# Projection stage of a graph network: carried rows weighed in place, GpSimd without its wait for VectorE

## The reference

```
alpha = softmax over the edges of a node (per head, 8 heads of 32 features)
out   = segment_sum(xs[src] * alpha)            # [6250, 256]
out   = out @ Wo + bo + b
out   = layernorm(out) * lg + lb + x            # x: the layer's input
then  batch norm over the nodes: mean and variance of each column
```

## Time and profile before

| | us |
|---|---|
| median of 3 timed runs | 8060.63 (8050.53 to 8062.14) |
| span of the profiled execution (the page gives no time around it) | 8042.1 |
| busy: PE, DVE, POOL, ACT | 5804.3, 4583.5, 4597.4, 2363.1 |
| projection stage, layer 1, between 1566.5 and 1789.0 | 222.5 |
| projection stage, layer 2, between 3064.0 and 3276.5 | 212.5 |

### The profile page before, as it was taken

The page is one execution under the profiler, slowest core; times in us unless marked ns, Lnnn a source line. Parts: engine busy times, 40 slices in busy tenths (PEclk is TensorE's granted clock), DMA queues, the critical chain, the costliest instruction groups (busy, mean ns, idle before and its releaser), DMA issues. The chain is left out here.

```text
span 8042.1 us, 109715 instructions
## 1 busy us (share of the span) xinstructions
PE 5804.3 (72%) x22914; PEld 3937.3 (49%) x23071; DVE 4583.5 (57%) x9420; ACT 2363.1 (29%) x7394; POOL 4597.4 (57%) x4150
## 2 busy tenths in 40 slices
PE   3699989688999978577776998565565666666640
PEld 2365555356666655466666444444444433334320
DVE  4577777766777776734444222444457444444438
ACT  0366666245666642200000111000002222222212
POOL 0277777215777742077776000777761888888870
PEclk7799999788998877655555899777777888888875
DMA  1745455115454532311111333555542666666664
GB/s 49 173 133 136 134 137 135 54 57 168 134 135 135 135 88 60 91 31 31 31 31 28 105 121 118 134 131 131 131 112 77 68 69 69 68 69 68 68 95 159
DMA packets 537478, 783.86 MB, mean 97 GB/s; under 512 B 92084, under 2 KB 410117, under 8 KB 535966
## 3 DMA queue, kind: packets, MB, share of 16 engines
q0 software_dynamic: 269440, 489.53, 31.7%
q1 hardware_dynamic: 266542, 291.49, 11.9%
q10 hardware_dynamic: 1348, 1.21, 0.0%
HBM read 531.97 MB, written 249.93 MB: 97 GB/s over the span
## 5 line engine op out<-in xcount | busy, mean ns | idle before, releaser
L725 POOL DMA_INDIRECT at_x<-table,at_idx x1664 | 1590.7, 956 | 673.4 <-issue 516.5
L2545 POOL DMA_INDIRECT acc<-sc_rows,sc_idx x832 | 1355.6, 1629 | 298.1 <-DMA acc<-sc_rows,sc_idx 180.6
L1954 POOL DMA_INDIRECT rel_ring<-rel_table,rel_idx x784 | 741.0, 945 | 845.7 <-ACT rel_idx L2000 607.3
L800 PE MATMUL at_psO<-at_x,at_main 128*128 128x273 f32 x3328 | 1063.0, 445 | 125.6 <-DVE agg L990 123.4
L1797 POOL DMA_INDIRECT conv_x<-conv_table,conv_idx x784 | 755.5, 964 | 389.4 <-issue 238.6
L2585 PE MATMUL sc_psR<-gated,sc_pick 128*128 x1664 | 592.3, 452 | 459.9 <-ACTq L2623 457.0
L1982 PE MATMUL rel_psO<-rel_ring,rel_hot 128*128 x1664 | 606.3, 543 | 423.7 <-issue 217.0
L990 DVE TENSOR_TENSOR agg<-agg,at_psO 128x273 f32 x1664 | 726.8, 437 | 246.5 <-DVE agg L990 167.0
L800 PEld LDWEIGHTS at_psO<-at_x,at_main 128*128 128x128 f32 x3328 | 621.6, 205 | 496.4 <-issue 369.4
L1982 PEld LDWEIGHTS rel_psO<-rel_ring,rel_hot 128*128 128x128 f32 x1664 | 462.6, 285 | 567.8 <-issue 466.6
L2585 PEld LDWEIGHTS sc_psR<-gated,sc_pick 128*128 128x128 f32 x1664 | 296.1, 210 | 752.7 <-issue 743.9
(11 more groups left out here) (431 smaller groups left out, 9329.8 us busy)
## 6 DMA issues: line engine op xcount, KB each, us to landing
at_place<-places SPq DMA_DIRECT2D x208, 256.0 KB, 3.7
rel_table<-cr_rows SPq DMA_DIRECT2D x50, 1024.0 KB
at_x<-table,at_idx POOLq DMA_INDIRECT x1664
acc<-zeros SPq DMA_DIRECT2D x204, 128.5 KB
la_t<-acc SPq DMA_DIRECT2D x40, 642.5 KB
acc<-sc_rows,sc_idx POOLq DMA_INDIRECT x832, 3.9
pj_x<-table SPq DMA_DIRECT2D x20, 640.0 KB, 4.2
conv_x<-conv_table,conv_idx POOLq DMA_INDIRECT x784, 2.4
```

What stands on the lines that cost most here:

```text
L725: pool.indirect_dma_start(x[b][:, j, 0:TABW], None, d.table[0:NR, :], bass.IndirectOffsetOnAxis(ap=idx[b][:, j:j + 1], axis=0)).then_inc(x ...
L800: ins = nc.tensor.matmul(psO[j % BANKS][:, 0:AGG], main[b % 2][:, j, :], x[b][:, j, 0:AGG], start=True, stop=True)
L1954: pool.indirect_dma_start(x[:, at:at + D], None, d.rel_table[:, :], bass.IndirectOffsetOnAxis(ap=idx[r][:, j:j + 1], axis=0)).then_inc(x_r ...
L2545: pool.indirect_dma_start(d.acc[k][0:NR + P, :], bass.IndirectOffsetOnAxis(ap=idx[b][:, j:j + 1], axis=0), rows[b % 2][:, j, :], None, com ...
```

## The change

`s2` and `sq` are gone. The carried rows are multiplied in place, in the carried table, and POOL no longer waits for `sum_ready` ahead of them. L1371 adds the table's rows. The squares go into the table's first five rows and `mean` and `var` into two rows of its second chunk, which have been read by then. The waits ahead of the squares stay.

```
-        s2 = sb("s2", [P, CT, D])
-        sq = sb("sq", [P, CT, D])
...
-        mean, var = s2[:, 0, :], s2[:, 1, :]
         cg = cagg[:].rearrange("p (n k) -> p n k", k=AGG)
+
+        sq = cg[:, 0:CT, 0:D]
+        mean, var = cg[:, CT, 0:D], cg[:, CT + 1, 0:D]
...
                 def carried_rows(c):
-                    if c >= 1:
-                        pool.wait_ge(sum_ready, c)
-                    nc.gpsimd.tensor_tensor(heads(s2[:]), heads(cg[:, c * CT:(c + 1) * CT, 0:D]), f(c, 1), ALU.mult).then_inc(carried, 1)
+                    rows = heads(cg[:, c * CT:(c + 1) * CT, 0:D])
+                    nc.gpsimd.tensor_tensor(rows, rows, f(c, 1), ALU.mult).then_inc(carried, 1)
...
-                    v.tensor_tensor(s1[b][:], s1[b][:], s2[:], ALU.add).then_inc(sum_ready, 1)
+                    v.tensor_tensor(s1[b][:], s1[b][:], cg[:, cs, 0:D], ALU.add).then_inc(sum_ready, 1)
```

## The result

The changed kernel takes 8099.2 us (median of 4 runs, 8088.7 to 8100.4) where the kernel before takes 8061.0 (median of 4): **1.0046 of before, 95% interval 1.0031 to 1.0060**, slower by 38 us. In a second comparison it was 1.0052 (1.0038 to 1.0066), 41 us.

What follows compares the result with a forecast made beforehand. VectorE's sum was taken as the path, GpSimd's wait as slack. Meetings in weigh(4) to weigh(8) and long returns gave +25.1 a layer, +50.2 for two: span 8092.3, with 18.5 to the median 8111 us, range 8085 to 8140.

Steps and rivals of the forecast that it cites:

- The burst is hidden: Carried rows 2 to 5 run back to back from 1589.6 to about 1598.9; at most one VectorE operation loses 2.2, covered by 5 us.
- L1370 of before pays 2.57: In weigh(4) to weigh(8), a shift starting 4.46 after a finish makes this sum take 4.06, +2.57.
- The next sum pays 2.2: In weigh(4) to weigh(7), the carried row queued behind the shift goes ahead of L1371, which loses 2.2.
- rival A: In weigh, L1371 goes ahead of the waiting carried row, only the shift costs: +16.3 a layer, 8093; chance 0.14.
- D: Not slower: loads of h land 6.7 or more after a finish, shifts meet nothing, down to 8053; chance 0.08.
- Turn(20) at 1647.86: Layer 1: weigh(4) ends at 1647.86 instead of 1643.09, so this PE turn comes 3.26 late.
- Turn(25) at 1669.31: Layer 1: this PE turn follows the factors at 1652.99 by 11.55 + 4.77.
- Each return 6.19: From PE's turn over PE and ScalarE to VectorE's next factors: 6.19 every time, nearly all at 1.2 GHz.
- rival B: PE's clock stays at 2.4 GHz, each return but the last is 3.64: +14.9 a layer, 8090; chance 0.09.
- Turn(25): PE stands 4.1: Layer 1: PE would reach this turn at 1665.19 and stand 4.1, about the gap followed by half clock.
- Rival C: PE's clock doesn't come back, its tiles take 5.34 and set the pace: +46.3 a layer, 8153; chance 0.07.
- The 18.5 between the span and the median: The kernel before: timed median 8060.6 lies 18.5 above the profiled span; left as is and added to the forecast span.

## Why the prediction was right, and where it was off

The forecast was 8111, slower by 50; measured was slower by 38 and 41, and by 43.9 in the two stages of the profile. The mechanism came as forecast, and one term of the sum was too large. Of the 12 us between 8111 and 8099, 6.3 lie in the two stages; the rest is the distance between the stages of one execution and the medians, and isn't traced further. Step by step:

- *The wait is slack, the sum is the path*: held; with the wait in place the rest of the change makes no difference that shows.
- *The burst is hidden*: held. Its price fell on another operation than I thought: L1380, a small tensor_scalar, took 1.30 instead of 0.17 at 1600.67, and weigh(2) began 1.3 late. PE's turn(10) came without a wait.
- *L1370 of before pays 2.57*: held to 0.01 (4.06). *The next sum pays 2.2*: it pays 2.02 (3.51), and GpSimd goes first, as forecast; rival A falls. So does D, since the shifts of weigh(4) to weigh(8) start 4.27 to 5.14 after a finish, not 6.7.
- *Turn(20) at 1647.86*: it came at 1650.96 on this trace's clock, 3.11 late from the start, so 1647.85. *Turn(25) at 1669.31*: 1669.17.
- *Each return 6.19*: this is the term that was mis-sized. The five returns of the changed kernel's profile in layer 1, as rows of L1385:

```profile
1675.91 0.19 DVE L1385 RECIPROCAL pj_rs<-pj_rs 128x5 f32<-128x5 f32 x1 [3.69 <-ACT pj_rs L1489]
...
1698.39 0.19 DVE L1385 RECIPROCAL pj_rs<-pj_rs 128x5 f32<-128x5 f32 x1 [6.24 <-ACT pj_rs L1489]
...
1718.15 0.19 DVE L1385 RECIPROCAL pj_rs<-pj_rs 128x5 f32<-128x5 f32 x1 [3.68 <-ACT pj_rs L1489]
...
1737.20 0.19 DVE L1385 RECIPROCAL pj_rs<-pj_rs 128x5 f32<-128x5 f32 x1 [4.97 <-ACT pj_rs L1489]
...
1757.52 0.19 DVE L1385 RECIPROCAL pj_rs<-pj_rs 128x5 f32<-128x5 f32 x1 [6.24 <-ACT pj_rs L1489]
```

  Two short, one between, two long. Counted from PE's turn, as in the prediction, they are 3.63, 6.19, 3.62, 4.92 and 6.19, so 2.56 + 2.57 + 1.27 = 6.4 less than five times 6.19. The cheaper carried rows give 0.3 more (L1369 of weigh(6) took 4.21 and used up part of it). The forecast of +25.1 at this L1385 came out as 1757.52 - 3.11 - 1736.04 = +18.4, 6.7 less. In layer 2 it was +22.7 (one return of 4.90, the others 6.24 and 6.25), and 2.6 more came from the tail, behind the last weigh, where shift_h(9) met finish(8) and hadn't before. In the second profile of the same kernel the last four returns of layer 1 are all long. So rival B holds in some chunks of some executions, and the right price was a mean of 4.9 to 5.9, not the longest. The trace of before had shown a third length, 5.32 at 1699.34, which the prediction passed over.
- *Turn(25): PE stands 4.1*: it stood 1.22. PE reached this place late, since the clock was still low: its tiles from turn(21) on came 5.3 apart (1654.59, 1659.88, 1665.16). That cost nothing, VectorE was later still. The sign "4 us or more at turn(25) to turn(45)" came at turn(30) alone, 5.87; the others were 1.22, 3.10, 3.70 and 3.35.
- *Rival C* falls: after the long return at 1692.20 PE's tiles came 5.3 apart twice and then 2.9 and 2.8. But the row that the prediction sets against it doesn't show the clock back: the turn at 1735.19 still takes 0.64, as at half clock. The granted clock is 0.50 up to it and 0.70 from there to 1736.04.
- *The 18.5 between the span and the median* wasn't time around the span. Where a run lists both, they lie 1.6 apart (8100.4 and 8098.8); the profiled execution of before was simply a quick one. The difference of the stages was the right thing to add to the median, and that is what the sum did.

Still open is what sets a single return. After the shortest stand of PE the return is short, after the longest it is long, but in between the stands don't order them, as PE's timeline of the changed kernel shows (stand in brackets):

```profile
1672.28 0.44 PE L1428 MATMUL pj_psT<-ident,pj_s 128*128 128x128 f32 x2 [1.22 <-DVE pj_s L1370]
...
1692.20 0.69 PE L1428 MATMUL pj_psT<-ident,pj_s 128*128 128x128 f32 x2 [5.87 <-DVE pj_s L1370]
...
1714.53 0.44 PE L1428 MATMUL pj_psT<-ident,pj_s 128*128 128x128 f32 x2 [3.10 <-DVE pj_s L1370]
...
1732.28 0.44 PE L1428 MATMUL pj_psT<-ident,pj_s 128*128 128x128 f32 x2 [3.70 <-DVE pj_s L1370]
...
1751.33 0.69 PE L1428 MATMUL pj_psT<-ident,pj_s 128*128 128x128 f32 x2 [3.35 <-DVE pj_s L1370]
```

The windows view of the last three returns, as above:

```profile
1714.53:1718.15 3.62, 3.62 (x16) 2.49 (x16) 0.00 (x0) 1.78 (x6) 0.00 (x0) 1.00 0.65 181
1732.28:1737.20 4.92, 4.92 (x15) 3.40 (x16) 0.00 (x1) 1.79 (x6) 0.00 (x0) 0.66 0.00 0
...
1751.33:1757.52 6.19, 6.19 (x15) 4.06 (x16) 0.01 (x1) 1.79 (x6) 0.00 (x0) 0.50 0.01 3
```

After stands of 3.10, 3.70 and 3.35 the returns are 3.62, 4.92 and 6.19. The return follows the clock: 1.00 is 2.4 GHz throughout, 0.50 is 1.2 GHz, 0.66 a mean of the two. The clock doesn't follow the stand's length alone. The trace of before had shown that too, in layer 2, where two stands of almost one length have a long and a short return behind them:

```profile
3191.99 0.44 PE L1429 MATMUL pj_psT<-ident,pj_s 128*128 128x128 f32 x2 [1.12 <-DVE pj_s L1371]
...
3208.79 0.44 PE L1429 MATMUL pj_psT<-ident,pj_s 128*128 128x128 f32 x2 [1.05 <-DVE pj_s L1371]
```

The next L1386 came at 3197.24 and 3212.42, 5.25 and 3.63 later, at mean clocks of 0.67 and 1.00.

## What to carry to other kernels

A wait that is slack for its own engine may still be what keeps two engines apart. Before you take it away, list what runs in its shadow (here a shift queued behind the waiting operation) and where that will start instead: on the path, a GpSimd operation that reads beside a VectorE operation with two inputs costs VectorE nearly the whole of the other's time. When an engine is freed, give its work a new place in another's idle time: with the carried rows early, the kernels whose shifts wait were 16 to 19 us faster than before, the one whose shifts run free 27 slower.

## What the runs showed of the hardware that I had not expected

A VectorE tensor_scalar on 5 words, with one input tensor, was held by the burst too: L1380 took 1.30 instead of 0.17 and ended with the burst (1600.67 + 1.30 = 1601.97; 1591.47 + 10.47 = 1601.94). The bn_stats ahead of it ran beside the same burst unhindered (1.73 for five, as without it), and so does the reciprocal beside a shift in the kernel before. The Trainium skill (SBUF — State Buffer, Who interferes with whom) names tensor_scalar among the operations that can take the pair of ports which VectorE shares with GpSimd; this row agrees.

GpSimd is held as well, and the rows fit a taking of turns: shift, L1369, carried row, L1370, each whole. From the end of L1367 in weigh(4), 1641.78 + 1.49 = 1643.27, to that of L1370, 1650.90, are 7.63 us, not much under the four own times one behind the other (2.88 + 1.49 + 2.34 + 1.49 = 8.20); the shift had started 0.86 earlier. The order is worked out from starts and lengths, no row shows it directly.
